# A four-layer graph network on one core: how layer 2's unit boundary is copied out, and where its side work stands

## The reference

```python
h = einsum('bnc,hdc->bhnd', x, Wh)                 # 4 heads of 64
s = einsum('...nd,...md->...nm', h, h)             # dot products
attn = softmax(where(mask, s, -1e16), axis=-1)
out_h = einsum('...nm,...md->...nd', attn, h) + bh
z = leaky_relu(concat_heads(out_h), 0.2)
h2 = einsum('bnk,dk->bnd', z, Wo)                  # the "out" unit
out2 = the same attention on h2, + bo
z2 = leaky_relu(out2, 0.2)
out = (z2 - mean) * rsqrt(var + 1e-5) * gamma + beta
```

## Time and profile before

| | |
|---|---|
| Median of three runs | 1941.51 us (1940.23 to 1941.58) |
| The profiled execution | 1944.51 us, span of its instructions 1942.6 us |
| Mean granted TensorE clock | 0.990 |
| Busy in the span | PE 95%, PEld 80%, DVE 84%, ACT 65%, POOL 46% |
| Chain that ended last | PE 80%, POOL 7%, DVE 5%, ACT 4%, issue 3% |
| Layer 2 | from about 412.7 us to about 1735 us of the span |

### The profile page before, as it was taken

One profiled execution on the slowest core, in us unless ns is written; L12 is line 12 of the kernel. 1 busy time (PEld: TensorE's weight loads), 2 busy tenths in 40 slices (PEclk: granted clock), 3 DMA queues, 4 the chain that ended last, 5 costly groups with the idle time before them and its releaser, 6 DMA issues.

```text
span 1942.6 us, 91782 instructions
## 1 busy us (share of the span) xinstructions
PE 1852.7 (95%) x42280; PEld 1555.5 (80%) x42280; DVE 1637.3 (84%) x1946; ACT 1271.3 (65%) x1955; POOL 900.7 (46%) x670
## 2 busy tenths in 40 slices
PE   7998899999999999999999999999999999989998
PEld 6777799978877878787777877878777777867887
DVE  6999999668888888888888888888888888868998
ACT  4887677347677676777777777776767777644332
POOL 5677899622243443424344243443424344254753
PEclk7999999999999999999999999999999999999999
DMA  7000000011111112121111111111111111101111
GB/s 187 4 4 4 3 2 3 2 30 39 32 29 35 35 36 35 35 35 35 35 35 35 30 34 34 33 35 36 35 35 35 35 35 35 36 2 25 26 28 34
DMA packets 134320, 61.01 MB, mean 31 GB/s; under 512 B 122416, under 2 KB 122672, under 8 KB 133936
## 3 DMA queue, kind: packets, MB, share of 16 engines
q1 hardware_dynamic: 131712, 54.55, 13.6%
q10 hardware_dynamic: 2224, 0.59, 0.1%
HBM read 8.98 MB, written 4.19 MB: 7 GB/s over the span
## 4 chain that ended last, share of the span: by engine, by line
PE 80%; POOL 7%; DVE 5%; ACT 4%; issue 3%; DMA 0%; ACTq 0%; POOLq 0%; DVEq 0%
PE ACC L1676 36%; PE S L1855 27%; PE S L1834 8%; PE AX L1902 3%; DVE ring L1305 3%; POOL st_rstd L555 1%; PE AX L1875 1%; PE AX L1656 1%; PE AX L1666 1%; POOL zt L846 1%; POOL zt L849 1%; ACT st_x L906 1%; PE S L1733 1%; ACT st_x L898 1%; POOL zt L843 1%
## 5 line engine op out<-in xcount | busy, mean ns | idle before, releaser
L1676 PEld LDWEIGHTS ACC<-V,ring 128*64 128x64 f32 x28672 | 973.0, 138 | 208.9 <-issue 95.7
L1676 PE MATMUL ACC<-V,ring 128*64 128x65 f32 x28672 | 989.5, 223 | 58.1 <-issue 33.3
L1451 DVE TENSOR_TENSOR ring<-ring,mask_self_t 128x1024 f32<-128x1024 f32 x640 | 847.3, 1328 | 146.8 <-ACT ring L1067 146.1
L1067 ACT ACTIVATE ring<-S,dot_bias 128x1024 f32<-128x1024 f32 x640 | 712.3, 1113 | 329.4 <-PE S L1855 311.7
L1855 PE MATMUL S<-FA 128*64 128x512 f16 x5120 | 675.2, 381 | 3.0 <-DVE o L1440 3.0
L1855 PEld LDWEIGHTS S<-FA 128*64 128x64 f16 x5120 | 290.8, 111 | 129.0 <-issue 13.0
L1305 DVE SCALAR_TENSOR_TENSOR ring<-S,pair_q,mask_t 128x1024 f32<-128x1024 f32 x256 | 315.1, 1272 | 16.6 <-DVE f_max L1317 4.3
L804 POOL TENSOR_TENSOR EV_both<-score,recip 128x512 f32<-128x512 f32 x64 | 123.5, 1930 | 266.5 <-DVE score L1460 266.4
L1834 PE MATMUL S<-parts,mask_t 128*128 128x128 bf16 x3072 | 172.0, 219 | 1.6 <-DVE o L1440 1.4
L1834 PEld LDWEIGHTS S<-parts,mask_t 128*128 128x128 bf16 x3072 | 171.6, 98 | 2.0 <-issue 2.0
L797 POOL TENSOR_TENSOR V<-v_plain,bh_bc 128x512 f32<-128x512 f32 x64 | 101.3, 1583 | 99.8 <-ACT v_plain L1092 99.8
(11 more groups left out here) (140 smaller groups left out, 1880.9 us busy)
## 6 DMA issues: line engine op xcount, KB each, us to landing
FA<-FA SPq DMA_DIRECT2D x160, 128.0 KB, 2.3
X<-in_x SPq DMA_DIRECT2D x16, 256.0 KB, 5.0
ring<-in_adj SPq DMA_DIRECT2D x8, 512.0 KB, 8.7
out_x<-X SPq DMA_DIRECT2D x16, 256.0 KB, 2.6
FA<-HL SPq DMA_TRANSPOSE x80, 3.0
wh<-in_wh_t ACTq DMA_DIRECT2D x2, 64.0 KB, 6.8
bh_bc<-in_bh ACTq DMA_DIRECT2D x1, 128.0 KB, 9.7
w_gat<-in_w_gat ACTq DMA_DIRECT2D x4, 16.0 KB, 3.6
```

Source lines behind the costliest of these rows:

```text
L1067: act.activation(ring[:, jt, :], S[jt % 2][:, :], ACT.Exp, bias=dot_bias[:, n % 2:n % 2 + 1])\
L1451: dve.tensor_tensor(ring[:, jt, :], ring[:, jt, :], mask_self_t[:, jt, :], ALU.mult)\
L1676: last = pe.matmul(acc_of(t)[rows, :], ring[:, jt, t * P + c * CUT:t * P + (c + 1) * CUT], values, start=(jt == 0 and t % 4 == 0), stop=(j ...
```

## The change

It touches layer 2 only. On ACT the copy of the accumulator becomes two activations, one for each bank. The first waits for a new semaphore `pv_half`, which PE raises when the last tile's sums of the first bank are complete, and raises `acc_half`; the second waits for `pv_done` and raises `acc_copied`. On PE the next unit's tile-0 sums wait for `acc_half` ahead of the first bank and for `acc_copied` ahead of the second. `squares` of the next unit moves behind this copy (from tile 1 to tile 2). The squares and roots of the norms move by one or two tiles. On PE the turn of heads 0 and 1 (`turn_heads(b, 0)`) moves in head 3 from tile 7 to tile 2, `turn_next` in head 2 from tile 5 to tile 2 (save for b = 0), `turn_heads(b - 1, 1)` in head 0 from one block at tile 6 to two halves at tiles 6 and 7, both on `AX` bank 1, and `spread_bound` from tile 3 to tile 5. On DVE `norms` moves from tile 1 to tile 3 and `bias` from tile 4 to tile 6. The last two units and layers 0, 1 and 3 stay as they were.

```diff
         for u in UNITS[:-1]:
             if after(u):
                 place_values(after(u))
+            if is_head(u, 3) and u is not BEFORE:
+                place_pair("Z", u["b"], 0)
+            if after(u):
                 place_bound(after(u))
             if is_head(u, 0) and u["b"] > 0:
-                place_pair("Z", u["b"] - 1, 2)
+                place(("Z", u["b"] - 1, 2), 1)
+                place(("Z", u["b"] - 1, 3), 1)
             if is_head(u, 2) and u["b"] + 1 < B:
                 place_norm(2, u["b"] + 1)
             if u is BEFORE:
                 place_norm(3, 0)
                 place_peak(3, 0)
                 place_norm(3, 1)
-            if is_head(u, 3):
+            if u is BEFORE:
                 place_pair("Z", u["b"], 0)
         place_nodes(3, 0)
         place_peak(3, 1)
...
             def sums(u):
-                act.wait_ge(pv_done, T * (dot_unit_of(u["n"]) + 1))
                 if u["n"] == 0:
                     act.wait_ge(gat_o, B)
                 else:
                     act.wait_ge(z_epi, 3 * u["n"])
                 if u is LAST:
                     act.wait_ge(gat_o, B + FIRST)
-                copy_acc()
+                act.wait_ge(pv_half, u["n"] + 1)
+                act.activation(accs_4d[:, 0], acc_all[:, 0], ACT.Copy).then_inc(acc_half, 1)
+                act.wait_ge(pv_done, T * (dot_unit_of(u["n"]) + 1))
+                act.activation(accs_4d[:, 1], acc_all[:, 1], ACT.Copy).then_inc(acc_copied, 1)
             def values(u):
...
                 act.wait_ge(on_dve, 4 * n + 4)
                 act.activation(on_rstd[:, :], on_ve[:, :], ACT.Exp, scale=-0.5).then_inc(on_pool, 1)
-            def turned(b, chunk):
-
-                for q in (2 * chunk, 2 * chunk + 1):
+            def turned(b, chunk, halves=(0, 1)):
+
+                for half in halves:
+                    q = 2 * chunk + half
                     k, at = AX_AT["Z", b, q]
                     act.wait_ge(ax_full[k], at + 1)
                     act.activation(z_t[:, chunk, (q % 2) * HALF:(q % 2 + 1) * HALF], AX[k][:, :], ACT.Copy)\
...
                     values(after(u))
                 if jt == LAG - 1 and 0 < u["n"] < LAST["n"]:
                     sums(UNITS[u["n"] - 1])
-                if jt == 1 and after(u):
+                if jt == LAG - 1 and after(u):
                     squares(after(u))
-                if jt == 2 and is_head(u, 1) and b + 1 < B:
+                if jt == 3 and is_head(u, 1) and b + 1 < B:
                     ln_squares(b + 1)
-                if jt == 1 and is_head(UNITS[u["n"] - 1], 1) and u["n"] > 0 and b_of(u) + 1 < B:
+                if jt == 3 and is_head(UNITS[u["n"] - 1], 1) and u["n"] > 0 and b_of(u) + 1 < B:
                     ln_root(b_of(u) + 1)
-                if jt == 3 and is_head(u, 2) and b > 1:
+                if jt == 4 and is_head(u, 2) and b > 1:
                     stat_squares(b - 2)
-                if jt == 1 and is_head(u, 3) and 0 < b < B - 1:
+                if jt == 3 and is_head(u, 3) and u is not BEFORE:
+                    turned(b, 0)
+                if jt == 4 and is_head(u, 3) and 0 < b < B - 1:
                     out_squares(b - 1)
-                if jt == 5 and is_head(u, 3) and 0 < b < B - 1:
+                if jt == 6 and is_head(u, 3) and 0 < b < B - 1:
                     out_root(b - 1)
-                if jt == 6 and is_head(u, 0) and b > 0:
-                    turned(b - 1, 1)
-                if jt == 6 and is_head(u, 2) and b + 1 < B:
+                if jt >= 6 and is_head(u, 0) and b > 0:
+                    turned(b - 1, 1, (jt - 6,))
+                if jt == (3 if b > 0 else 6) and is_head(u, 2) and b + 1 < B:
                     turned_norm(b + 1)
-                if jt == 7 and is_head(u, 3):
+                if jt == 7 and u is BEFORE:
                     turned(b, 0)
             def first_features():
...
             def epilogue(u):
+                dve.wait_ge(acc_half, u["n"] + 1)
                 dve.wait_ge(acc_copied, dot_unit_of(u["n"]) + 1)
                 if u is LAST:
                     dve.wait_ge(gat_o, B + FIRST)
...
             def dot_unit(u, jt):
                 b, nxt = u["b"], after(u)
-                if jt == (2 if b < B - 1 else 0) and is_head(u, 3) and b > 0:
+                if jt == (4 if b < B - 1 else 0) and is_head(u, 3) and b > 0:
                     out_var(b - 1)
                 if jt == 0 and nxt:
                     feature_rest(nxt)
-                if jt == 1 and nxt:
-                    norms(nxt)
                 if jt == 2 and 0 < u["n"] < LAST["n"]:
                     epilogue(UNITS[u["n"] - 1])
-                if jt == 4 and nxt:
+                if jt == 3 and nxt:
+                    norms(nxt)
+                if jt == 6 and nxt:
                     bias(nxt)
                 if jt == 6 and is_head(u, 0) and b + 1 < B:
                     ln_mean_of(2, b + 1)
...
                 n, jt = divmod(m, T)
                 if jt == 0:
                     pe.wait_ge(v_made, n + 1)
-                    pe.wait_ge(acc_copied, dot_unit_of(n))
-                weigh(dot_tile_of(m), jt, V[:, n % 3, jt, 1:D + 2])
-
-            def turn_heads(b, chunk):
+                    if 0 < n < LAST["n"]:
+                        pe.wait_ge(acc_half, n)
+                    else:
+                        pe.wait_ge(acc_copied, dot_unit_of(n))
+                pe.wait_ge(weight_done, dot_tile_of(m) + 1)
+                for t in range(T):
+                    if jt == 0 and t == T // 2:
+                        pe.wait_ge(acc_copied, dot_unit_of(n))
+                    for c in range(2):
+                        rows = slice(c * CUT, (c + 1) * CUT)
+                        last = pe.matmul(acc_of(t)[rows, :], ring[:, jt, t * P + c * CUT:t * P + (c + 1) * CUT],
+                                         V[:, n % 3, jt, 1:D + 2], start=(jt == 0 and t % 4 == 0), stop=(jt == T - 1),
+                                         skip_group_check=True)
+                    if jt == T - 1 and t == T // 2 - 1:
+                        last.then_inc(pv_half, 1)
+                last.then_inc(pv_done, 1)
+
+            def turn_heads(b, chunk, halves=(0, 1)):
                 last_head = next(u["n"] for u in UNITS if is_head(u, 2 * chunk + 1) and u["b"] == b)
                 pe.wait_ge(z_epi, 3 * last_head + 3)
-                for q in (2 * chunk, 2 * chunk + 1):
+                for half in halves:
+                    q = 2 * chunk + half
                     k = take_bank(AX_AT["Z", b, q])
                     for t in range(4):
                         row = 4 * (q % 2) + t
...
                 b = u["b"]
                 if jt == 0 and after(u):
                     values(after(u))
-                if jt == 3 and after(u):
+                if jt == 2 and is_head(u, 3) and u is not BEFORE:
+                    turn_heads(b, 0)
+                if jt == (2 if b > 0 else 5) and is_head(u, 2) and b + 1 < B:
+                    turn_next(b + 1)
+                if jt == 5 and after(u):
                     spread_bound(after(u))
-                if jt == 6 and is_head(u, 0) and b > 0:
-                    turn_heads(b - 1, 1)
-                if jt == 5 and is_head(u, 2) and b + 1 < B:
-                    turn_next(b + 1)
-                if jt == 7 and is_head(u, 3):
+                if jt >= 6 and is_head(u, 0) and b > 0:
+                    turn_heads(b - 1, 1, (jt - 6,))
+                if jt == 7 and u is BEFORE:
                     turn_heads(b, 0)
             def first_features():
```

More of the change, by code:

```diff
@@ L242, in gnn_stack @@
         pv_done = sem("pv_done")
+        pv_half = sem("pv_half")
+        acc_half = sem("acc_half")
         acc_copied = sem("acc_copied")
```

## The result

The changed kernel takes **1916.87 us** (median of four runs, 1916.77 to 1917.57); the kernel before, run beside it, 1941.55. The ratio is 0.9875, its 95% interval 0.9858 to 0.9892: 24.7 us faster, where 36.1 were forecast, and 2.4 us above the range. The profiled execution took 1916.88, its span is 1915.1 us and its mean clock 0.992, so for after the profile stands at the median.

The account below looks back on a forecast made before the run. Layer 2 was taken as bound by PE's own stream plus its waits. Boundary stalls of 42.0 us, less 1.5, 3.9 and 0.45, gave 36.1 us off the median of 1941.5: 1905.4 us, range 1900 to 1914.5.

Parts of the forecast that it names:

- The boundaries: PE's stalls before the first sums at five unit boundaries: 2.80 us a cycle, 15 x 2.80 = 42 us in all.
- the covers at out and head 3: Out: ACT's exponential of tile 3 has 1 us spare; head 3: transposes give ACT 1.1 us, so 1.14 comes back.
- the turns' cover: Transposes between last sums and next dots in heads 2 and 3 give ACT time, closing stalls of 0.22 and 1.14 us.
- Copy by halves: ACT's half copy takes 0.38 us, so the stalls of 0.18 and 0.20 us at heads 0 and 1 close.
- the other estimate, 0.52: Half copy by the skill page's budget: 0.52 us, about 0.10 us kept at each tight boundary, the sum 3 us worse.
- The residual of 0.05 at heads 0 and 1: Stall of 0.05 us left at each of these two boundaries for the tight fit: 30 x 0.05 = 1.5 us.
- The split turn: Head 0's turn of heads 2 and 3 as two blocks of 4 costs PE 0.26 us in 15 graphs, 3.9 us.
- Later norms: Moved norms, bound and bias add no work; norms are ready 0.4 us before PE's spread in head 0.
- the second rival: POOL late for head 0's turn, partly through work slowed beside DVE: PE loses 7.5 us, 1913 us; chance 0.05.
- Norms late for the spread: Rival: norms 0.5 us late for PE's spread in three of five units, 22 us lost, 1928 us; chance 0.07.
- the first two rivals: Small boundary stalls stay, 1914.3 us, chance 0.17; POOL late for head 0's turn, 1913 us, chance 0.05.
- The end of layer 2: PE waits for POOL before layer 3's first norm; the bias now goes ahead of that chain: +0.45 us, once.

Follow-up runs that it names:

- e5: Changed kernel with the next unit's norms on DVE behind tile 2's mask product, ahead of the epilogue: 1901.67 us.
- e9: e5 with the accumulator copied in one activation again instead of by halves: 1914.11 us.
- e4: Changed kernel with the turn of heads 2 and 3 as one block of 8 transposes behind tile 7 of head 0: 1915.2 us.
- e12: e10 with DVE's bias behind tile 5 instead of tile 6: 1900.35 us.
- e10: e5 with the turn of heads 2 and 3 in one block behind tile 7: 1909.63 us.
- e6: Changed kernel with POOL's gamma and beta operations of the out norm cut to 64 of 512 columns: 1901.54 us, one execution.
- e1: Changed kernel with out_root on ACT put back behind tile 5 of head 3 instead of tile 6: 1907.61 us.

## Why the prediction missed

The direction was right and the gain too large. Distances between PE's starts over one cycle account for all of it. From before to after:

| PE's distances, summed over a cycle | before | after | difference |
|---|---|---|---|
| dots to sums, 40 | 37.43 | 34.68 | -2.75 |
| sums to spread and spread to dots, 5 each | 5.87 | 6.96 | +1.09 |
| turns of `z`: to them, behind them, and sums to dots elsewhere | 31.19 | 31.37 | +0.18 |
| everything else | 8.60 | 8.56 | -0.04 |
| cycle | 83.09 | 81.57 | -1.52 |

*The boundaries.* 2.80 a cycle forecast, 2.75 measured (2.75 in e5 too). The order of ACT's work, the covers at out and head 3 and the turns' cover all held.

*Copy by halves.* Forecast 0.38, measured 0.38 and 0.39. The 0.3 us behind the other estimate, 0.52, are given by the Trainium skill's page "ScalarE: Activation LUTs" (section "Rules for kernel authors") for an activation whose bias is a pointer operand. This copy has no such bias, so the comparison in the prediction says nothing against the page. The residual of 0.05 at heads 0 and 1 was not there: 0.10 a cycle on the safe side. e9 shows what the halves are worth in this order, 0.65 a cycle.

*The split turn.* 0.26 forecast, 0.18 measured against before. Against one block in the new order the split costs 0.3 (0.14 and a wait of 0.16 in e4, 0.20 and 0.11 in e12). Whether one block gives that back depends, by e4, e10 and e12, on who holds bank 0; the text did not ask it.

*Later norms: the step that failed.* The text says "Cover: 0.4 us, and as much in head 1 and the out unit", with the norms ready 4.1 us behind head 0's first sums (1064.21 to 1068.3) and PE there at 4.5. PE wanted the spread at 1051.43 + 0.93 = 1052.36, 4.52 behind the sums. The norms were ready at 1053.36, 5.52 behind them: 1.4 us later than worked out. The sum took DVE as waiting for ACT's exponential, with a product of 1.33 behind it. In fact DVE comes to that product late: the exponential is done at 1049.52 and the product starts at 1051.36, since the epilogue alone runs 1.01 us over its 0.64, and `HL` ahead of it 1.08 over its 0.68. Where POOL is out of the way, in e6, the sum comes out: ready at 3.9. In head 1 the same cover was used up too, by 0.1 us, and neither e1 nor e6 changes that. There it is the product ahead of the norms, which starts within POOL's divide of the unit before and takes 2.03 us:

```profile
1068.52 2.03 DVE L1462 TENSOR_TENSOR ring<-ring,mask_self_t 128x1024 f32<-128x1024 f32 x1 [0.18 <-ACT ring L1073]
```

```profile
1068.41 1.04 POOL L810 TENSOR_TENSOR EV_both<-score,recip 128x512 f32<-128x512 f32 x1 [3.85 <-DVE score L1472]
```

In the out unit the cover held.

*POOL, where the cause was in the sum but not its effect.* POOL was followed for what it delivers, and that came out: the divide was to end 5.25 us behind head 0's first sums (1068.3 against 1064.39 - 1.34), in after it ends at 1053.47, 5.63 behind; the turn did not wait for it. What DVE has to do while POOL is busy was not asked. It had to be, since the earlier trace rows show a mean of 1327 ns for a product, and the second rival speaks of work "slowed beside DVE", only the other way about.

*The rivals.* "Norms late for the spread" was the right mechanism with a chance of 0.07. It was priced at three units of five with 0.5 us each, 1.5 us a cycle; it was 1.06 in one and 0.1 in another, together the 1.16 by which e5's cycle is shorter than after's (81.57 - 80.41). The range reached only to the first two rivals; with this one in it, it would have held. The bias was late in after, in one unit: the text has it ready about 0.3 us ahead of the next unit's first exponential in head 1, and that exponential waited 0.73 us for it, about the same in all 14 cycles:

```profile
1010.61 1.11 ACT L1073 ACTIVATE ring<-S,dot_bias 128x1024 f32<-128x1024 f32 x1 [0.73 <-DVE dot_bias L1501]
```

The forecast cover of about 1.3 us behind it was enough: in all of layer 2 PE's dots wait 0.3 us for an exponential.

*The end of layer 2.* +0.45 forecast, +0.39 measured.

*The sum again.* The forecast cycle was shorter by 2.44, the measured one by 1.52. The 0.92 between them are +1.09 at the spread, +0.05 at the boundaries, -0.10 for the residual, -0.08 for the turn, -0.04 for the rest. Over 15 cycles 0.92 make 13.8 us, which would put the median at 1905.4 + 13.8 = 1919.2; it is 2.3 lower. That part lies outside the steady cycles and was not traced to a place; the first dots of layer 2 alone start anywhere between 404.5 and 409.2 us in the fourteen traces, though no kernel changes anything ahead of them.

## What to carry to other kernels

When a change moves an operation of GpSimd, list what VectorE does in the stretch where it lands, and give each of its operations with two SBUF inputs that starts within one of GpSimd the worst case, GpSimd's remaining time plus its own; a mean over a group hides this (823 ns for 642 or 1650). Put on the vector queue first what the matmul engine waits for, even where it is "ready in time": that move of one line was worth 15 us here. And when a wait is handed on instead of vanishing, look at who holds the buffer: three experiments failed on a bank that a small operation, queued behind large ones, had not yet released.

## What was not expected of the hardware

An operation of VectorE with two SBUF inputs that starts within a 128x512 operation of GpSimd ends about its own time, less 0.1 us, after it, however early it started: 0.68 became 1.76, 0.64 became 1.65 and a 128x1024 product of 1.2 became 1.89. It works the other way too: POOL's addition to the values took 1.94 us where it started within a product, and 1.28 where it did not (at 1029.03 in after). A reduction with one input kept its 0.68 us, and POOL's root over 8 columns, 2.10 us long, stretched neither of the two products beside it.
